# A query product with the cosine and sine parts stacked in its rows instead of a block-diagonal one

## The chip, the cores and the metric

One core of a Trainium2 chip runs the whole program. The metric is device time in microseconds, the median of the timed runs. PE is TensorE (PEld its weight loads), DVE VectorE, ACT ScalarE, POOL GpSimd and SP SyncE, which here issues DMAs.

## The reference, cut to what matters

The program is two decoder layers: RWKV mixing, a cross-attention over 1601 context rows and a mixture of experts, then grouped attention, a latent cross-attention and a second mixture. The change lies in the first cross-attention. What it computes for its queries:

```
q_hk  = (hidden_q @ Wq.T).reshape(B, S, H=16, K=128)
q_big = einsum('bshk,hkq->bshq', q_hk, w_kc_q)            # 192 dims a head
q_big = q_big * cos_q + rotate_half(q_big) * sin_q
q_r   = einsum('bshq,hqr->bhsr', q_big, W_qr)              # 64 dims a head
k_r   = einsum('bld,hdr->bhlr', kv_r, W_kr)
scores = einsum('bhsr,bhlr->bhsl', q_r, k_r)
```

The kernel folds Wq with w_kc_q (W1) and W_qr with W_kr (W2), so that the scores are a product of a 64-dim query per head with kv_r itself. The rotation is turned round: instead of rotating the 192 dims and multiplying by W2, it multiplies them by cosines and sines and uses W2 and W2 with its halves exchanged.

## The kernel before

**Heads go in pairs.** There are 8 pairs. A pair's 2 x 192 = 384 dims lie in three tiles of 128 partitions: tile 0 is the first 128 dims of its first head, tile 1 the first 128 of its second, tile 2 the last 64 of the first head (partitions 0 to 63) and the last 64 of the second (64 to 127). The tokens, 1024, go in two halves of 512 columns. So there are 16 jobs, n = 2 x pair + half.

**A job.** `z_jobs(n)` on PE makes the three tiles (`z`) in a bank each, from W1 and the normalised x, both split into a high and a low part (three products each, and two blocks of 128 channels: 18 products of 128x128 by 512). `rotate(n)` on DVE reads each bank and writes `zc` = z times cosine and `zs` = z times sine. `q_job(n)` on PE makes the query of both heads in one bank: partitions 0 to 63 are the first head's, 64 to 127 the second's. For tiles 0 and 1 it uses products of half the array's width (64 columns), one per head and part. For tile 2, which holds both heads, it uses `W2[:, p, c, 128:256]`, a 128x128 block-diagonal matrix, once with `zc` and once with `zs`. ACT copies the query's high part into `QALL`, `lows(n)` on DVE subtracts it and leaves the low part in `qlo`, and SP moves that by DMA into the other half of `QALL`'s partitions.

**The order.** Each engine's instructions are in the order of the program. On PE it is z(0), then z(n+1), q(n) for each n, with the turned keys (`first_keys`) ahead of q(14). On DVE it is rotate(0), then rotate(n+1), lows(n), with four low parts of the keys behind rotate(15). PSUM has 8 banks, taken in turn; a job waits until the one 8 banks back has been emptied.

**How W2 is made** (the end of the first stage, lines 615 to 629 and 1241 to 1254). `W2E` holds, for each pair, the product of W_kr and W_qr with 192 dims and the first 32 again, so that both the plain and the exchanged half are slices of it. For each pair PE turns two slices of 128 columns and, with four small products with the identity, puts the two heads' last 64 dims on the diagonal. ACT copies this out in three pieces per pair, four pairs ahead of `deviations(1, 1)` (the root for the second half of the layer norm) and four behind it. POOL has cleared the rest of the block-diagonal part with a memset. Then PE turns the normalised x (`turn_x(1)`), ACT takes its high part (`z_HTh`) and DVE its low part (`z_HTl`), all engines meet (`ended`), and the jobs start.

After the 16 jobs comes the unit stage (scores, softmax, context for 32 units), whose first scores wait for the last queries.

Of the kernel before, what the change touches and what calls it, by code (L numbers as in the profile page):

```python
# [13 lines left out]
P = 128  # L14
# [5 lines left out]
ALU = mybir.AluOpType  # L20
ACT = mybir.ActivationFunctionType
# [10 lines left out]
D = 64  # L32
H = 16
PAIRS = H // 2
QW = 192
# [51 lines left out]
def decoder(nc, x, ctx_512, L0_attn_Wk, L0_attn_Wv, L0_attn_Wr, L0_attn_Wo, L0_attn_time_decay, L0_attn_time_first,  # L87
# [5 lines left out]
    with ExitStack() as ctx:  # L93
# [5 lines left out]
        def sem(name):  # L99
            return ctx.enter_context(nc.semaphore(name))  # L100
# [12 lines left out]
        def at(name, offset, shape, dt=F32):  # L113
            size = int(np.prod(shape[1:])) * 4
            assert offset + size <= room, (name, offset + size, room)
            return nc.alloc_sbuf_tensor_at(name, shape, dt, offset=arena + offset)
# [38 lines left out]
        WkrT = at("WkrT", 40960, [D, H * D])  # L155
        x_woT = at("x_woT", 145152, [P, H, C])
        W1 = at("W1", 65536, [P, KC, H * QW])
        W2 = at("W2", 104480, [P, PAIRS, 2, 256])
        cosq = at("cosq", 129056, [P, 3, HALF])
        sinq = at("sinq", 135200, [P, 3, HALF])  # L160
        zc = at("zc", 141344, [P, 2, 3, HALF])
# [212 lines left out]
        w_exp = sem("rwkv_exp_ready")  # L374
        decay_exp = sem("decay_exp_ready")
        rw_ready = sem("rwkv_mixed")
        w2_cleared = sem("folded_weights_cleared")
        decay_set = sem("decays_ready")
        scan_step = sem("decayed_sums_ready")
        eps_added = sem("denominators_guarded")  # L380
# [126 lines left out]
        def _(pe):  # L507
            def begin(key, by):
                ps = banks.claim(key, by)
                if banks.earlier(key) is not None:  # L510
                    pe.wait_ge(*banks.emptied(banks.earlier(key)))
                return ps
# [103 lines left out]
            for t in range(NT):  # L616
                out_product(("ro", t), [(r_num[:, ct, t * P:(t + 1) * P], r_wt[:, 3, ct, :]) for ct in range(KC)])
            pe.wait_ge(*banks.emptied(("w2t", 3)))
            for p in range(PAIRS):
                ps = begin(("w2", p), "act")  # L620
                for c, (whole, rest) in enumerate(((0, P), (QW // 2, 32))):
                    o = 256 * c
                    nc.tensor.transpose(ps[:, o:o + P], W2E[:, p, whole:whole + P], ident[:, :])  # L623
                    for s in range(2):
                        rows = slice(s * D, (s + 1) * D)
                        last = mm(ps[rows, o + P + s * D:o + P + (s + 1) * D], W2E[rows, p, rest:rest + D], ident[rows, rows])
                last.then_inc(filled, 1)
            turn_x(1)
            ended(pe, 1)

# [10 lines left out]
            def q_job(n):  # L641
                p, half, s = n // 2, n % 2, n % 2
                pe.wait_ge(*banks.emptied(("z", p, half, 2)))
                ps = begin(("q", p, half), "dve")
                for c, r in enumerate((zc, zs)):
                    mm(ps[0:64, :], W2[:, p, c, 0:64], r[:, s, 0, :], c == 0, False, skip_group_check=True)
                    mm(ps[64:128, :], W2[:, p, c, 64:128], r[:, s, 1, :], c == 0, False, skip_group_check=True)
                for c, r in enumerate((zc, zs)):
                    last = mm(ps, W2[:, p, c, 128:256], r[:, s, 2, :], False, c == 1, skip_group_check=True)
                last.then_inc(filled, 1)  # L650

            def first_keys():

# [6 lines left out]
                    last.then_inc(filled, 1)  # L660

            wait_ht(1)
            banks.start_at(len(banks.order) % 8 + 4)
            z_jobs(0)
            for n in range(2 * PAIRS):
                if n + 1 < 2 * PAIRS:
# [488 lines left out]
        def _(act):  # L1155
# [82 lines left out]
            for g in range(4):  # L1238
                copy_out(("u", g), U[:, 2 * g:2 * g + 2, :])

            def folded(pairs):
                for p in pairs:
                    ps = banks.take(("w2", p), "act")
                    act.wait_ge(*banks.filled(("w2", p)))
                    src = ps.rearrange("p (c w) -> p c w", c=2)
                    nc.scalar.activation(W2[:, p, :, 0:P], src[:, :, 0:P], ACT.Copy)
                    nc.scalar.activation(W2[0:D, p, :, P:P + D], src[0:D, :, P:P + D], ACT.Copy)
                    nc.scalar.activation(W2[D:P, p, :, P + D:256], src[D:P, :, P + D:256], ACT.Copy).then_inc(emptied["act"], 1)

            deviations(1, 0)  # L1250
            act.wait_ge(w2_cleared, 1)
            folded(range(0, 4))
            deviations(1, 1)
            folded(range(4, PAIRS))
            for g in range(2):
                for kc in range(KC):
                    act.wait_ge(*banks.filled(("ht", 1, g, kc)))
# [214 lines left out]
        def _(dve):  # L1472
# [8 lines left out]
            V = nc.vector  # L1481
# [87 lines left out]
            def rotate(n):  # L1569
                p, half, s = n // 2, n % 2, n % 2  # L1570
                for j in range(3):
                    key = ("z", p, half, j)
                    ps = banks.take(key, "dve")
                    dve.wait_ge(*banks.filled(key))
                    if n >= 2:
                        dve.wait_ge(*banks.filled(("q", (n - 2) // 2, n % 2)))
                    V.tensor_tensor(zc[:, s, j, :], ps, cosq[:, j, :], ALU.mult)
                    V.tensor_tensor(zs[:, s, j, :], ps, sinq[:, j, :], ALU.mult).then_inc(emptied["dve"], 1)

            def lows(n):  # L1580
                p, half, s = n // 2, n % 2, n % 2
# [416 lines left out]
        def _(pool):  # L1998
# [19 lines left out]
            for ct in range(KC):  # L2018
# [1 line left out]
                for half in range(2):  # L2020
                    pool.wait_ge(*banks.emptied(("kvr", 2, ct, half)))
                G.tensor_tensor(r_sig[:, ct, :], r_num[:, ct, :], r_sig[:, ct, :], ALU.mult).then_inc(gated, 1)
            pool.wait_ge(*banks.emptied(("xwo", 7)))
            G.memset(W2[:, :, :, P:2 * P], 0.0).then_inc(w2_cleared, 1)

            def split(p):
                wide, narrow = slice(0, 2 * P), slice(2 * P, 3 * P)
                src = W1[:, :, 3 * P * p:3 * P * (p + 1)].rearrange("p k (h q) -> p k h q", h=2)
# [353 lines left out]
```

## Time and profile before

| | us |
|---|---|
| median of 3 runs | 1364.19 |
| lowest and highest | 1359.41, 1368.82 |
| span of the profiled execution | 1379.6 |
| PE busy in it | 1272.7 (92%) |
| DVE busy | 868.2 (63%) |
| POOL busy | 824.0 (60%) |
| ACT busy | 634.6 (46%) |

### The profile page before, as it was taken

What the parts mean: (1) busy time and instruction counts of PE and PEld (TensorE: products, weight loads), DVE (VectorE), ACT (ScalarE), POOL (GpSimd) and SP (SyncE); (2) the same over time, 40 slices, a digit from 0 to 9 for tenths busy, and PEclk for the clock granted to TensorE, in tenths of its full rate; (3) what the DMA queues carried; (4) which work ended last, traced back from release to release, by engine and by line L of the source; (5) the groups of instructions that cost most, each with busy time, mean ns of one, the idle gap of its engine ahead of it and who ended that gap; (6) DMA issues with size and microseconds to landing.
All of it is one profiled execution on the core that took longest, in us unless ns stands there. A gap on an engine that the chain in (4) does not pass through costs nothing.

```text
span 1379.6 us, 20358 instructions
## 1 busy us (share of the span) xinstructions
PE 1272.7 (92%) x7123; PEld 826.8 (60%) x7123; DVE 868.2 (63%) x1490; ACT 634.6 (46%) x1687; POOL 824.0 (60%) x748
## 2 busy tenths in 40 slices
PE   7999997999999999999999758998999999989792
PEld 4865554666666666666668643445776874556582
DVE  4756666677777777778865636675666123664443
ACT  3731123445554455544551416887665115872151
POOL 1267005799999999999993445887444004560444
PEclk9999997999999999999999888999999997998897
DMA  9501111000000000000005620000000105200263
GB/s 261 134 9 32 37 31 27 9 8 9 9 11 10 9 9 9 10 11 9 9 5 176 195 65 2 1 1 1 1 1 1 27 1 155 63 1 32 69 142 118
DMA packets 66172, 58.91 MB, mean 43 GB/s; under 512 B 19424, under 2 KB 62968, under 8 KB 65560
## 3 DMA queue, kind: packets, MB, share of 16 engines
q1 hardware_dynamic: 62952, 49.09, 12.7%
q0 software_dynamic: 3120, 8.52, 2.6%
q8 instruction: 58, 0.95, 0.3%
q14 instruction: 42, 0.34, 0.1%
HBM read 40.69 MB, written 8.52 MB: 36 GB/s over the span
## 4 chain that ended last, share of the span: by engine, by line
PE 79%; DVE 6%; ACT 5%; POOL 4%; issue 4%; DMA 1%; DVEq 0%; SPq 0%; POOLq 0%; ACTq 0%
PE PS L515 73%; PE PS L523 5%; ACT s_sc L1402 2%; POOL a_m L2137 2%; POOL a_m L2131 2%; DVE s_mx L1859 1%; ACT a_m L1356 1%; DVE pm L1622 1%; DVE HN L1504 0%; PE PS L729 0%; DMA f_xg<-token_rows,f_ids 0%; POOL s_sc L2152 0%; PE PS L685 0%; POOL f_xg L2119 0%; PE PS L623 0%
## 5 line engine op out<-in xcount | busy, mean ns | idle before, releaser
L2080 POOL TENSOR_TENSOR PWS<-PWS 128x1024 f32<-128x1024 f32 x160 | 379.7, 2373 | 45.1 <-ACT PWS L1286 25.8
L1622 DVE TENSOR_REDUCE pm<-PS 128x2 f32<-128x1024 f32 x192 | 225.8, 1218 | 69.3 <-PE PS L515 68.7
L1286 ACT ACTIVATE PWS<-PS 128x512 f32<-128x512 f32 (+1 forms) x416 | 213.3, 599 | 78.4 <-PE PS L515 78.2
L515 PE MATMUL PS<-PWS,KVR 128*64 128x256 f32 (+1 forms) x1664 | 185.8, 380 | 0.0
L515 PE MATMUL PS<-QALL,KH 128*128 128x512 f32 (+1 forms) x416 | 182.6, 439 | 0.9 <-DVE QM L1646 0.9
L515 PE MATMUL PS<-QM,KL 68*128 68x512 f32 (+1 forms) x416 | 167.3, 402 | 0.0
L2152 POOL TENSOR_SCALAR s_sc<-s_sc,s_ri 128x128 f32<-128x128 f32 (+1 forms) x256 | 104.5, 429 | 98.9 <-DVE s_ri L1866 98.9
L515 PEld LDWEIGHTS PS<-PWS,KVR 128*64 128x64 f32 (+1 forms) x1664 | 121.4, 137 | 59.0 <-issue 0.9
L515 PEld LDWEIGHTS PS<-QALL,KH 128*128 128x128 f32 (+1 forms) x416 | 77.9, 187 | 76.9 <-ACT PWS L1286 57.4
L1402 ACT ACTIVATE s_sc<-PS,s_nb 128x128 f32<-128x128 f32 (+1 forms) x256 | 104.5, 433 | 3.9 <-DVE s_nb L1862 3.9
L1859 DVE TENSOR_REDUCE s_mx<-PS 128x2 f32<-128x512 f32 (+2 forms) x112 | 65.7, 611 | 50.1 <-PE PS L515 50.0
L515 PE MATMUL PS<-KH,QALL 64*128 64x512 f32 (+1 forms) x512 | 89.3, 408 | 7.0 <-DVE pm L1622 7.0
L515 PE MATMUL PS<-a_wT,HT 128*128 128x512 f32 x192 | 93.4, 620 | 0.7 <-issue 0.7
L1297 ACT ACTIVATE QALL<-CTX 128x256 fp32r<-128x256 f32 x32 | 13.3, 417 | 154.0 <-DVE CTX L1659 154.0
L515 PEld LDWEIGHTS PS<-QM,KL 68*128 68x128 f32 (+1 forms) x416 | 79.0, 190 | 6.2
L515 PEld LDWEIGHTS PS<-KH,QALL 64*128 64x128 f32 (+1 forms) x512 | 46.9, 189 | 43.7 <-issue 26.0
L515 PE MATMUL PS<-z_HTh,z_w 128*128 128x512 f32 x192 | 67.5, 420 | 2.4 <-DVEq L502 2.4
L2180 POOL DMA_INDIRECT e_x<-token_rows,e_ids x31 | 29.5, 951 | 67.2 <-DVE e_ids L1956 46.8
L2131 POOL TENSOR_TENSOR a_m<-a_m,a_m 128x512 f32<-128x512 f32 x40 | 51.0, 1276 | 29.5 <-DVE a_m L1836 29.5
L1271 ACT ACTIVATE QALL<-PS 64x512 fp32r<-64x512 f32 x32 | 19.0, 594 | 106.3 <-PE PS L515 105.9
L1525 DVE TENSOR_TENSOR X<-X,PS 128x256 f32<-128x256 f32 x40 | 16.8, 419 | 76.8 <-PE PS L515 76.7
L1390 ACT ACTIVATE s_pt<-PS 128x512 f32<-128x512 f32 x64 | 38.5, 602 | 53.6 <-PE PS L523 53.6
(328 smaller groups left out, 2518.3 us busy)
## 6 DMA issues: line engine op xcount, KB each, us to landing
QALL<-qlo SPq DMA_DIRECT2D x32, 128.0 KB, 2.4
QM<-QALL SPq DMA_DIRECT2D x64, 64.0 KB, 2.0
f_w<-in_L_ffn_w_dram SPq DMA_DIRECT2D x2, 2048.0 KB
tile_results<-e_y SPq DMA_DIRECT2D x31, 128.0 KB
a_nat<-in_L_attn_w_qkv_dram SPq DMA_DIRECT2D x1, 3072.0 KB, 13.0
x_wq<-in_L_xattn_Wq_dram SPq DMA_DIRECT2D x1, 2048.0 KB, 10.4
x_wo<-in_L_xattn_Wo_dram SPq DMA_DIRECT2D x2, 1024.0 KB, 6.9
a_wo<-in_L_attn_w_o_dram SPq DMA_DIRECT2D x1, 2048.0 KB, 17.5
```

Source lines behind the costliest of these rows:

```text
L515: return nc.tensor.matmul(o, a, b, start=start, stop=stop, **kw)
L523: last = nc.tensor.transpose(ps[0:w, c:c + r], a, ident[0:r, 0:r])
L1286: nc.scalar.activation(PW[c][0:rows, j * HALF:(j + 1) * HALF], st_bank("block", LT * u + lt)[0:rows, :], ACT.Exp).then_inc(p_ready, 1)
L1390: nc.scalar.activation(s_pt[:, m % 2, 0, :], ps, ACT.Copy).then_inc(emptied["act_turned"], 1)
L1402: ins = nc.scalar.activation(s_sc[:, k % 4, h, 0:nk], ps[:, j * nk:(j + 1) * nk], ACT.Exp, bias=s_nb[:, k % 3, h:h + 1], scale=scale, accu ...
L1622: V.tensor_reduce(pm[u % 2][:, :, i // 3, i % 3], src, AX, ALU.max).then_inc(nat_read, 1)
L1859: ins = V.tensor_reduce(s_mx[:, k % 3, i * per:(i + 1) * per], banks.bank(key)[:, 0:per * nk].rearrange("p (h k) -> p h k", h=per), AX, AL ...
L2080: G.tensor_tensor(ACC[:, :], PW[0][:, :] if i == 0 else ACC[:, :], PW[i + 1][:, :], ALU.add).then_inc(acc_step, 1)
L2131: G.tensor_tensor(a_m1[:, n % 6, :], a_m1[:, n % 6, :], a_m2[:, n % 2, :], ALU.add).then_inc(m_sum, 1)
L2137: G.tensor_tensor(m1, m1, a_bt[:, i, s, :].unsqueeze(1).to_broadcast([P, 4, P]), ALU.add).then_inc(qk_ready, 1)
L2152: ins = G.tensor_scalar(s_sc[:, n % 4, h, 0:nk], s_sc[:, n % 4, h, 0:nk], s_ri[:, n % 4, h:h + 1], 1.0, ALU.mult, ALU.mult)
L2180: G.indirect_dma_start(e_x[:, j % 8, :], None, xs1, IndirectOffsetOnAxis(ap=e_ids[:, j:j + 1], axis=0)).then_inc(tile_back[j % 8], 16)
```

## The change

The last two products of `q_job`, of full width, become two of half width. Each head has its own weights for tile 2, with 128 rows: 64 for the cosine part and 64 for the sine part (`W2R[:, head, p, :]`). So the second index of `zc` and `zs` at tile 2 changes its meaning: `zc[:, s, 2, :]` holds the first head's cosine part in partitions 0 to 63 and its sine part in 64 to 127, and `zs[:, s, 2, :]` the second head's. `rotate` writes them with four instructions on 64 partitions each, two of which write other partitions than they read. W2's turned slices are made four to a bank and copied out whole, the small products write two banks of their own (one per head, cosine above sine), and the memset goes. `banks.start_at(4)` gives the same first bank as the expression that it replaces.

```
             for t in range(NT):
                 out_product(("ro", t), ...)
             pe.wait_ge(*banks.emptied(("w2t", 3)))
+            for g in range(4):
+                turn(("w2", g), "act", [W2E[:, p, whole:whole + P] for p in (2 * g, 2 * g + 1) for whole in (0, QW // 2)])
+            rests = [begin(("w2r", s), "act") for s in range(2)]
             for p in range(PAIRS):
-                ps = begin(("w2", p), "act")
-                for c, (whole, rest) in enumerate(((0, P), (QW // 2, 32))):
-                    o = 256 * c
-                    nc.tensor.transpose(ps[:, o:o + P], W2E[:, p, whole:whole + P], ident[:, :])
-                    for s in range(2):
-                        rows = slice(s * D, (s + 1) * D)
-                        last = mm(ps[rows, o + P + s * D:o + P + (s + 1) * D], W2E[rows, p, rest:rest + D], ident[rows, rows])
-                last.then_inc(filled, 1)
+                for s, ps in enumerate(rests):
+                    rows = slice(s * D, (s + 1) * D)
+                    for c, rest in enumerate((P, 32)):
+                        last = mm(ps[c * D:(c + 1) * D, p * D:(p + 1) * D], W2E[rows, p, rest:rest + D], ident[rows, rows])
+            last.then_inc(filled, 2)
...
-                for c, r in enumerate((zc, zs)):
-                    last = mm(ps, W2[:, p, c, 128:256], r[:, s, 2, :], False, c == 1, skip_group_check=True)
-                last.then_inc(filled, 1)
+                mm(ps[0:64, :], W2R[:, 0, p, :], zc[:, s, 2, :], False, True, skip_group_check=True)
+                mm(ps[64:128, :], W2R[:, 1, p, :], zs[:, s, 2, :], False, True, skip_group_check=True).then_inc(filled, 1)
...
             deviations(1, 0)
-            act.wait_ge(w2_cleared, 1)
-            folded(range(0, 4))
+            for g in range(4):
+                copy_out(("w2", g), W2[:, 2 * g:2 * g + 2, :, :])
             deviations(1, 1)
-            folded(range(4, PAIRS))
+            for s in range(2):
+                copy_out(("w2r", s), W2R[:, s, :, :])
...
-                    V.tensor_tensor(zc[:, s, j, :], ps, cosq[:, j, :], ALU.mult)
-                    V.tensor_tensor(zs[:, s, j, :], ps, sinq[:, j, :], ALU.mult).then_inc(emptied["dve"], 1)
+                    if j < 2:
+                        V.tensor_tensor(zc[:, s, j, :], ps, cosq[:, j, :], ALU.mult)
+                        V.tensor_tensor(zs[:, s, j, :], ps, sinq[:, j, :], ALU.mult).then_inc(emptied["dve"], 1)
+                        continue
+                    for h, both in enumerate((zc, zs)):
+                        mine = slice(h * D, (h + 1) * D)
+                        V.tensor_tensor(both[0:D, s, j, :], ps[mine, :], cosq[mine, j, :], ALU.mult)
+                        ins = V.tensor_tensor(both[D:P, s, j, :], ps[mine, :], sinq[mine, j, :], ALU.mult)
+                    ins.then_inc(emptied["dve"], 1)
...
-            pool.wait_ge(*banks.emptied(("xwo", 7)))
-            G.memset(W2[:, :, :, P:2 * P], 0.0).then_inc(w2_cleared, 1)
```

## Rows read from the trace of the kernel before

**Rows 1.** The page, chain that ended last, share of the span by engine.

```profile
PE 79%; DVE 6%; ACT 5%; POOL 4%; issue 4%; DMA 1%; DVEq 0%; SPq 0%; POOLq 0%; ACTq 0%
```

**Rows 2.** Busy time by stretches (stretch, length, PE, PEld, DVE, ACT, POOL, clock, DMA).

```profile
82.00:210.00 128.00, 127.92 (x495) 74.33 (x497) 81.80 (x130) 19.60 (x35) 47.86 (x49) 1.00 0.14 29
```

**Rows 3.** Timeline of DVE and ACT in the jobs (start, duration, engine, line, operation).

```profile
97.68 0.68 DVE L1578 TENSOR_TENSOR zs<-PS,sinq 128x512 f32<-128x512 f32 x1
98.28 0.68 DVE L1577 TENSOR_TENSOR zc<-PS,cosq 128x512 f32<-128x512 f32 x1
...
100.07 0.68 DVE L1578 TENSOR_TENSOR zs<-PS,sinq 128x512 f32<-128x512 f32 x1
...
102.23 1.21 ACT L1271 ACTIVATE QALL<-PS 64x512 fp32r<-64x512 f32 x2 [6.62 <-PE PS L515]
...
103.47 1.39 DVE L1589 TENSOR_TENSOR qlo<-PS,QALL 64x512 fp32r<-64x512 f32 x2 [2.73 <-ACT QALL L1271]
...
110.12 1.21 ACT L1271 ACTIVATE QALL<-PS 64x512 fp32r<-64x512 f32 x2 [6.67 <-PE PS L515]
```

**Rows 4.** Timeline of PE over the query products of job 1.

```profile
98.34 1.08 PE L515 MATMUL PS<-zc,W 128*64 128x512 f32 x4
99.25 1.03 PE L515 MATMUL PS<-zs,W 128*64 128x512 f32 x4
100.21 1.12 PE L515 MATMUL PS<-zc,W 128*128 128x512 f32 x2
...
102.26 0.40 PE L515 MATMUL PS<-z_HTl,z_w 128*128 128x512 f32 x1
```

**Rows 5.** Timeline of PE's weight loads there.

```profile
101.60 0.19 PEld L515 LDWEIGHTS PS<-z_HTh,z_w 128*128 128x128 f32 x1 [0.24 <-issue]
102.03 0.19 PEld L515 LDWEIGHTS PS<-z_HTl,z_w 128*128 128x128 f32 x1 [0.24 <-issue]
```

**Rows 6.** Timeline of PE, turned keys and query products of jobs 14 and 15.

```profile
200.78 1.53 PE L659 MATMUL PS<-ident,DUP 128*128 128x128 f32 x13
...
202.24 1.08 PE L515 MATMUL PS<-zc,W 128*64 128x512 f32 x4
...
206.02 1.08 PE L515 MATMUL PS<-zc,W 128*64 128x512 f32 x4
```

**Rows 7.** Line 1646, DVE's row maxima (durations in ns, least, median, most).

```profile
L1646 DVE TENSOR_TENSOR QM<-PS,ident x32: 681/682/683, 219.9 to 710.0; 4x512 fp32r<-4x512 f32 x32
```

**Rows 8.** The chain that ended last in order of time, folded weights.

```profile
70.01 0.26 PE PS L623
70.27 0.26 PE PS L515 x4
```

**Rows 9.** Timeline of the end of the first stage.

```profile
72.40 0.36 DVE L1498 BATCH_NORM_AGGREGATE mv<-stats 128x2 f32<-128x6 f32 x4
74.55 0.30 ACT L1171 ACTIVATE rstd<-mv,guard 128x4 f32<-128x4 f32 x1
75.10 1.38 DVE L1504 TENSOR_SCALAR HN<-X,mv,rstd 128x256 f32<-128x256 f32 x4
77.75 1.97 PE L523 MATMUL PS<-ident,HN 128*128 128x128 f32 x16
79.35 2.48 DVE L1565 TENSOR_TENSOR z_HTl<-PS,z_HTh 128x512 fp32r<-128x512 f32 x4 [2.87 <-ACT z_HTh L1258]
```

**Rows 10.** Timeline of PE, products of 64 rows by 64 columns.

```profile
56.12 2.82 PE L515 MATMUL PS<-WqrT,WkrT 64*64 64x192 f32 x32
```

**Rows 11.** Groups of instructions from 58 to 69.2 us.

```profile
L1167 ACT ACTIVATE U<-PS 128x512 f32<-128x512 f32 x4 | 2.4, 622 | 0.5 <-PE PS L515 0.5
```

**Rows 12.** Busy time by stretches, columns as in rows 2.

```profile
80.00:82.00 2.00, 0.00 (x0) 0.00 (x0) 1.83 (x4) 0.78 (x2) 0.06 (x1) 1.00 0.00 0
...
214.00:216.00 2.00, 0.56 (x2) 0.29 (x2) 1.97 (x3) 0.00 (x0) 1.63 (x3) 0.50 0.27 57
...
230.00:232.00 2.00, 2.00 (x8) 1.43 (x7) 0.00 (x0) 1.57 (x3) 1.86 (x2) 0.79 0.00 0
```

More of the change, by code:

```diff
@@ L157, in decoder @@
         W1 = at("W1", 65536, [P, KC, H * QW])
-        W2 = at("W2", 104480, [P, PAIRS, 2, 256])
+        W2 = at("W2", 104480, [P, PAIRS, 2, P])
+        W2R = at("W2R", 112672, [P, 2, PAIRS, D])
         cosq = at("cosq", 129056, [P, 3, HALF])
@@ L376, in decoder @@
         rw_ready = sem("rwkv_mixed")
-        w2_cleared = sem("folded_weights_cleared")
         decay_set = sem("decays_ready")
@@ L662, in _ @@
             wait_ht(1)
-            banks.start_at(len(banks.order) % 8 + 4)
+            banks.start_at(4)
             z_jobs(0)
@@ L1239, in _ @@
                 copy_out(("u", g), U[:, 2 * g:2 * g + 2, :])
[L1241 to L1248, printed above, removed]
             deviations(1, 0)
-            act.wait_ge(w2_cleared, 1)
-            folded(range(0, 4))
+            for g in range(4):
+                copy_out(("w2", g), W2[:, 2 * g:2 * g + 2, :, :])
             deviations(1, 1)
-            folded(range(4, PAIRS))
+            for s in range(2):
+                copy_out(("w2r", s), W2R[:, s, :, :])
             for g in range(2):
```

## The prediction

> **What bounds the kernel now.** I began with the chain that ended last. TensorE (PE) holds 79% of the span, so an edit pays if it shortens PE's own work where PE is that chain [rows 1]. Then the table by stretches: from 82 to 210 us, where the queries are made (call it the query stage), PE is busy 127.92 of 128.00 us at a granted clock of 1.00, while VectorE (DVE) has 81.80, ScalarE (ACT) 19.60 and GpSimd (POOL) 47.86 [rows 2]. The other three engines have room there and PE has none. Last, the timeline of one job, and that of the end of the stage before, from 69 to 82 us.
>
> The query stage is 16 jobs. ACT's copy of a finished query starts at 102.23 and again at 110.12, so a job lasts 7.89 us [rows 3]. On PE a job is 18 rotation-input products (z) and one query product group (q).
>
> Before, a job has two pairs and two full-width products, eight slots. After, it has three pairs, six slots. The new pair is of the same shape as those of the row (128 rows by 64 columns, two different moving tiles, one bank). Gain: 2 x 0.43 = 0.86 a job. The changeover from half to full width moves from inside q to between q and z, at the same price. At the end q jobs 14 and 15 stand one behind the other, 3.78 us apart (202.24 to 206.02) [rows 6]; there eight slots are 3.44 and the other 0.34 is two changeovers, most of which goes, and half of it goes behind the last job. Sum: 16 x 0.86 = 13.8, and 0.4, is 14.2 us.
>
> **What DVE pays.** The rotation by cosine and sine is six instructions of 128x512 a job. They start 0.60 us apart (97.68, 98.28) though one lasts 0.68: neighbours overlap. The two low-part instructions of 64x512 take 1.39 together, so these don't overlap: 0.69 each [rows 3]. After, the third z has four instructions of 64x512 where it had two of 128x512. I bound one by the row nearest in shape, 0.69 without overlap, and by 0.60 with it. Two of the four read 64 partitions and write the other 64. The one row that moves partitions is that of the row maxima, from partitions 0 to 3 into 64 to 67, 512 elements: 0.682 us, no dearer [rows 7]. DVE's job: 4 x 0.60 and 4 x 0.69 and 1.39 and two gaps of 0.03, 6.6 us, against 5.0 before. PE's job will be 7.89 - 0.86 = 7.03. DVE still waits 0.4 us a job for ACT, where it waited 2.73 (100.07 plus 0.68, to 103.47). Nor does it delay PE by order: rotation n+2 follows the low parts of n, which start 1.44 behind q job n, and so ends 1.44 + 6.6 = 8.0 us after it, while q job n+2 needs it 7.03 + 4.1 = 11.1 after it. So I cost DVE at nothing; the cover is 3 us of lead, and 0.4 us a job by throughput. If the cover goes, each 0.1 us of DVE's excess is 1.6 us in all.
>
> The Trainium skill (VectorE: DVE Perf Modes, Two Vector instructions with no wait between them) speaks against the change here: an instruction whose input or output starts in another group of 32 partitions than that of its neighbour starts only when everything earlier has finished. The trace agrees: 0.69 for the low parts, which step from partition 0 to 64, and 0.60 for the rotations. By it three of the four new instructions are held, as I have them; without it DVE's job would be 6.25 us.
>
> The end of the query stage is tighter. Counted from the start of the last z job, that is the end of q job 13, the last rotation ends at 1.44 + 1.39 + 5.2 = 8.0. PE has the z job (7.89 less the 3.69 from 98.34 to 102.03, 4.2), the turned keys (202.24 less 200.78, 1.46, [rows 6]) and q job 14 (six slots, 2.6) before q job 15, which it could start at 8.3. I charge nothing and keep 0.3 in the range.
>
> **The folded weights, 69 to 82 us.** PE alternates between a 128x128 turn, 0.26 us on the chain, and a group of four 64x64 records, 0.26 too, 16 times: 8.3 us [rows 8]. Two turns of x's halves, 16 records, take 1.97 [rows 9]: 0.12 apiece, so 0.14 of each 0.26 is the change of shape. After, the 16 turns stand together: 16 x 0.12 = 1.9. The 64 small records stand together as well. From below: 32 records of 64x192 take 2.82 us [rows 10], 0.088 each, a third of that for 64 columns is 0.03, so 1.9 us. From above: 0.26 per four, 4.2 us. The lower is nearer, since 0.26 holds the change of shape; I take 2.4. PE would then be through at 69.4 + 1.9 + 2.4 = 73.7 instead of 77.7.
>
> It doesn't all come out, for what is late next is the second half of the normalised rows. DVE has its variances at 72.76 and then waits until ACT, in the midst of its folded copies, turns to them at 74.55; the rows are written from 75.10 to 76.48 [rows 9]. After, ACT has four copies of 128x512 (0.622 each, [rows 11]) instead of twelve small ones: from 70.0 to 72.5, so the deviation goes at 72.8, the rows are ready at 74.7, PE's last turns end at 75.8, ACT's last high part at 76.9 and DVE's last low part at 77.7, where it was 79.35 + 2.48 = 81.83 [rows 9]. That is 4.1. With the small records at 4.2, PE ends them at 75.5, ACT's two copies of the rest follow, and the chain ends at 80.0: 1.8. I take 3.4, nearer to the first. The removed memset on POOL lay at 58.5 and kept nobody waiting: nil. No DMA is touched.
>
> **Sum.** 14.2 + 3.4 = 17.6 us of a span of 1379.6. The page gives the profiled execution's span alone; it is 15.4 above the median of the runs, 1364.19, and I carry the difference over: 1346.6. All that follows the query stage waits for PE's last q job or for what hangs on it and is the same code, so it moves up whole. What may differ is the clock there: the unit stage opens with gaps on PE and at 214 to 216 us the granted clock is 0.50, that is 1.2 GHz [rows 12]. How long it stays depends on how the gaps fall; the runs differ by 9 us with one kernel, and I put +-4 on it.
>
> **The rivals.**
> 1. *The third pair doesn't share its slots.* Then six half-width products cost eight slots, only the folded weights pay: 1364.2 - 3.4 = 1360.8. Against it stand the two pairs of [rows 4], of the same shape; for it, only that this pair closes the sum. 0.07.
> 2. *The clock falls before the query stage.* PE would now idle for the rows at 74 and again until 78. Before, it stood idle from 79.7 until DVE's last low part at 81.83 and the clock at 80 to 82 was 1.00 [rows 9, 12], which speaks against. In the unit stage it stayed at half from 214 to 231, 17 us; as much here costs 8.5: 1355. 0.08. [...]
> 3. *DVE becomes the bound, and the kernel slower.* The mechanism is the two instructions a job that move between partition halves. Beside them DVE's job is 6.6 - 1.4 = 5.2 us. It bounds above 7.03, so from 0.9 us for such an instruction. The kernel is slower than before when a job is 0.2 (the 3.4 of the first stage over 16) above 7.89, so from 1.4. At 1.8: 8.8 a job, 0.9 above, 16 x 0.9 - 3.4 = 11 slower, 1375. [rows 7] say 0.68 for a move of 64 partitions, but of four rows only, not of 64. 0.05. Short of that point, with DVE bound at 0.9 to 1.4, 1347 to 1361: 0.05.
> 4. *It does as said, and the sum holds*: 0.75, with 1341 to 1352 as its own range: the folded weights give -1.6 or +0.7, the last rotation 0.3, the clock and the median of few runs the rest.
>
> **Chances and range.** A measurement of this kernel can tell about 1%, 13.6 us, from no change: below 1350.5 is faster. Of case 4 nine tenths lie there, 0.68. Within 1%: the rest of 4, rivals 1 and 2, DVE bound short of slower, 0.27. Slower: 0.05. The range reaches from 1340 to 1356, case 4 and rival 2 with the nearer part of 3.
>
> **What would show it.** In the query stage ACT's query copies 7.03 us apart, not 7.9; in a q job twelve half-width records in six slots and no full-width one; DVE's four 64x512 instructions 0.69 apart and 0.3 to 0.5 us of waiting for ACT left before the low parts. In the first stage the 16 turns in 1.9 us and the last low part at 77.7 to 80. Wrong if a slot holds one half-width record in the new pair, if DVE's wait for ACT is gone, if the granted clock between 74 and 195 is under 1, or if the unit stage lengthens by what the query stage loses.

## The result, and the profile after

The changed kernel takes 1344.26 us (median of 4 runs, 1343.50 to 1354.52). The kernel before, on the same chip, takes 1366.51 (4 runs, 1359.41 to 1370.50). The ratio is 0.9869, 95% interval 0.9839 to 0.9900: 17.9 us of 1364, where 17.6 were forecast. It is not the quotient of the two medians, which is 0.9837, or 22.3 us; all ratios below are of this kind, and those of e1 to e4 leave out two executions of the kernel before that took 1822 and 3142 us. The profiled execution took 1343.5 us, with a span of 1341.7.

I read the two traces at landmarks first. Both kernels have the same code up to the folded weights and again from the first score product (KH by QALL) on. In the profiled executions these are the first z product, 82.08 before and 76.87 after, and the first score product, 209.80 and 193.46. So the first stage gave 5.2 us. Of these 0.8 are not the change's: PE starts the folded weights at 69.48 before and at 68.70 after, and the difference is there already at the first product of x_kcq by x_wq (38.64 and 37.86), in code that both share. The query stage went from 127.72 to 116.59, 11.1 less. From there to the end the code is the same. The two spans differ by 37.9, more than the medians do. The unit stage is 2.1 shorter, and the 19.5 that are left lie behind it, where the clock was lower in the profiled execution before: 0.68 from 1160 to 1180 us, 0.74 from 1260 to 1280 and 0.76 from 1300 to 1320, while the same code after, 18 to 38 us earlier, shows 1.00, 0.96 and 1.00. That part is none of the change's, and only the ratio of many runs is used for the whole.

In the chain that ended last PE holds 78% of the span, where it held 79% [rows 1].

PE over the query products of job 1 in the kernel after (the timeline; start, duration, engine, line, operation). It answers to [rows 4]:

```profile
95.18 1.08 PE L515 MATMUL PS<-zc,W 128*64 128x512 f32 x4
...
96.94 0.59 PE L515 MATMUL PS<-zc,W2R 128*64 128x512 f32 x1
...
96.95 0.59 PE L515 MATMUL PS<-zs,W2R 128*64 128x512 f32 x1
...
97.37 0.59 PE L515 MATMUL PS<-zc,W2R 128*64 128x512 f32 x1
97.38 0.59 PE L515 MATMUL PS<-zs,W2R 128*64 128x512 f32 x1
...
97.90 0.50 PE L515 MATMUL PS<-z_HTh,z_w 128*128 128x512 f32 x1
98.24 0.39 PE L515 MATMUL PS<-z_HTl,z_w 128*128 128x512 f32 x1
```

The third pair is seen at once: its records start two by two, 0.01 us apart, and the next two 0.43 later. From the first query record to the second z product of the next job it is 3.06 us (95.18 to 98.24), with twelve half-width records. Before it was 3.92 (98.34 to 102.26 [rows 4]), with eight half-width and four full-width ones: 0.86 more, two slots.

DVE and ACT in the same job (timeline of the kernel after), which answer to [rows 3]:

```profile
95.50 0.68 DVE L1570 TENSOR_TENSOR zs<-PS,sinq 128x512 f32<-128x512 f32 x1
...
96.10 0.67 DVE L1574 TENSOR_TENSOR zc<-PS,cosq 64x512 f32<-64x512 f32 x1
...
96.79 0.69 DVE L1575 TENSOR_TENSOR zc<-PS,sinq 64x512 f32<-64x512 f32 x1
...
97.48 0.69 DVE L1574 TENSOR_TENSOR zs<-PS,cosq 64x512 f32<-64x512 f32 x1
...
98.02 1.21 ACT L1262 ACTIVATE QALL<-PS 64x512 fp32r<-64x512 f32 x2 [5.78 <-PE PS L515]
98.19 0.69 DVE L1575 TENSOR_TENSOR zs<-PS,sinq 64x512 f32<-64x512 f32 x1
...
99.26 1.39 DVE L1587 TENSOR_TENSOR qlo<-PS,QALL 64x512 fp32r<-64x512 f32 x2 [0.37 <-ACT QALL L1262]
...
105.06 1.21 ACT L1262 ACTIVATE QALL<-PS 64x512 fp32r<-64x512 f32 x2 [5.84 <-PE PS L515]
```

ACT's copies stand 7.04 us apart (98.02, 105.06), where it was 7.89. The four new instructions start 0.69 to 0.71 apart, and DVE still waits 0.37 for ACT (0.43 in the next job), where it waited 2.73. So PE is still the bound, but with a twentieth of a job to spare. The two of L1575 and L1574 that move 64 partitions to the other half cost no more than the two that don't.

The seam at the end, PE's query products 14 and 15 and the first scores, and DVE's last instruction of rotation 15 (timelines of the kernel after), answers to [rows 6]:

```profile
188.16 1.08 PE L515 MATMUL PS<-zc,W 128*64 128x512 f32 x4
...
189.74 0.69 DVE L1575 TENSOR_TENSOR zs<-PS,sinq 64x512 f32<-64x512 f32 x1
...
190.79 1.03 PE L515 MATMUL PS<-zc,W 128*64 128x512 f32 x4
...
193.46 0.87 PE L515 MATMUL PS<-KH,QALL 64*128 64x512 f32 x4
```

Job 15 follows job 14 after 2.63 us instead of 3.78. PE doesn't wait for the last rotation, which ends at 190.43, 0.36 before job 15 starts.

The end of the first stage in the kernel after (timeline), which answers to [rows 8, 9]:

```profile
68.70 1.91 PE L523 MATMUL PS<-ident,W2E 128*128 128x128 f32 x16
...
70.54 1.16 PE L515 MATMUL PS<-ident,W2E 64*64 64x64 f32 x64
...
71.63 0.36 DVE L1489 BATCH_NORM_AGGREGATE mv<-stats 128x2 f32<-128x6 f32 x4
71.64 1.09 PE L523 MATMUL PS<-ident,HN 128*128 128x128 f32 x8
72.02 0.30 ACT L1170 ACTIVATE rstd<-mv,guard 128x4 f32<-128x4 f32 x1 [0.62 <-DVE mv L1489]
...
72.57 1.38 DVE L1495 TENSOR_SCALAR HN<-X,mv,rstd 128x256 f32<-128x256 f32 x4
...
74.01 1.09 PE L523 MATMUL PS<-ident,HN 128*128 128x128 f32 x8 [1.28 <-DVE HN L1495]
...
75.33 1.29 DVE L1556 TENSOR_TENSOR z_HTl<-PS,z_HTh 128x512 fp32r<-128x512 f32 x2 [0.18 <-ACT z_HTh L1249]
...
76.87 0.76 PE L515 MATMUL PS<-z_HTh,z_w 128*128 128x512 f32 x1 [1.77 <-DVEq L502]
```

The 16 turns take 1.8 us (forecast 1.9) and the 64 small records 1.1 in all. PE has done the first eight turns of x's rows at 72.7. Then it stands twice, 1.28 us before the other eight and 1.77 before z. What is late now is DVE: its variances at 71.99, the rows from 72.57, the last low part from 75.33. ACT waits 0.62 for DVE there, and not DVE for ACT.

In the second of these waits, at 76.2 us, the clock fell. Busy time by stretches of the kernel after, columns as in [rows 2]:

```profile
74.00:76.00 2.00, 1.09 (x8) 0.86 (x8) 1.82 (x4) 1.35 (x3) 0.00 (x0) 1.00 0.00 0
76.00:78.00 2.00, 1.13 (x3) 0.97 (x4) 0.62 (x2) 0.00 (x0) 1.13 (x3) 0.54 0.00 0
78.00:80.00 2.00, 2.00 (x7) 1.51 (x6) 0.10 (x1) 0.00 (x0) 2.00 (x3) 0.50 0.00 0
80.00:82.00 2.00, 2.00 (x6) 1.61 (x5) 1.19 (x2) 0.00 (x0) 1.86 (x3) 0.50 0.00 0
82.00:84.00 2.00, 2.00 (x8) 1.52 (x8) 1.29 (x2) 0.00 (x0) 2.00 (x3) 0.75 0.00 0
84.00:86.00 2.00, 2.00 (x11) 1.63 (x9) 1.84 (x3) 0.00 (x0) 2.00 (x3) 1.00 0.00 0
86.00:188.00 102.00, 102.00 (x442) 59.95 (x441) 95.03 (x147) 17.24 (x30) 38.95 (x39) 1.00 0.18 37
```

The first z products run at 1.2 GHz until 83 us: PE is busy all the time, with 6 or 7 records in 2 us where it has 11 from 84 on. In the one profiled execution of the kernel before nothing of it is there, though PE stood still from 80 to 82 [rows 12]. This is rival 2, in a short form.

### The profile page after: what moved, and what is told of

It reads as the page before. It is cut to its first block, busy times and chain, and to the rows that moved or that the text cites. A ratio compares the mean times of both kernels' runs of the same rounds, so it can differ in the third digit from the quotient of the medians.

```text
span 1341.7 us, 20371 instructions
## 1 busy us (share of the span) xinstructions
PE 1241.2 (93%) x7123; PEld 811.9 (61%) x7123; DVE 890.9 (66%) x1522; ACT 630.1 (47%) x1669; POOL 821.2 (61%) x747
## 4 chain that ended last, share of the span: by engine, by line
PE 78%; DVE 6%; ACT 6%; POOL 5%; issue 3%; DMA 2%; DVEq 0%; POOLq 0%; SPq 0%; ACTq 0%
PE PS L515 72%; PE PS L523 5%; ACT s_sc L1393 2%; POOL a_m L2132 2%; POOL a_m L2126 2%; DVE s_mx L1857 2%; ACT a_m L1347 1%; POOL e_yg L2180 1%; DVE pm L1620 1%; DVE HN L1495 1%; PE PS L728 0%; DVE stats L1485 0%; DMA f_xg<-token_rows,f_ids 0%; POOL s_sc L2147 0%; ACT PWS L1277 0%
## 5 line engine op out<-in xcount | busy, mean ns | idle before, releaser
L1277 ACT ACTIVATE PWS<-PS 128x512 f32<-128x512 f32 (+1 forms) x416 | 212.7, 600 | 76.7 <-PE PS L515 75.2
L1653 DVE RECIPROCAL PS<-PS 128x256 f32<-128x256 f32 x32 | 55.9, 1747 | 6.6 <-PE PS L515 6.6
```

What stands on the lines that cost most here:

```text
L1277: nc.scalar.activation(PW[c][0:rows, j * HALF:(j + 1) * HALF], st_bank("block", LT * u + lt)[0:rows, :], ACT.Exp).then_inc(p_ready, 1)
L1653: V.reciprocal(sums, sums).then_inc(inv_ready, 1)
```

## The experiments

All were run beside the kernel before; times of different rows need not be from the same chip, so compare ratios. e1 to e4 are from one chip, e5 to e8 from a second, and e9 to e11 and the row of before from a third. e1 gives the last 64 dims of each head other weights, and e9 leaves out the stacking of the cosine and sine parts, so their queries are not the reference's. "z" is the start of the first z product; "stage" is from there to the first score product; "half" is how long the granted clock was 0.50 between 74 and 84 us. z, stage and half are of the one profiled execution.

| run | time (runs) | ratio, 95% | z | stage | half |
|---|---|---|---|---|---|
| before | 1364.02 (11) | | 82.1 | 127.7 | 0 |
| after | 1344.26 (4) | 0.9869, 0.9839 to 0.9900 | 76.9 | 116.6 | 6.8 |
| e1_wide_again | 1361.37 (10) | 0.9982, 0.9954 to 1.0010 | 76.9 | 129.1 | 3.4 |
| e2_columns_apart | 1360.28 (1) | | 75.9 | 129.2 | 3.4 |
| e3_shapes_mixed | 1349.29 (10) | 0.9903, 0.9871 to 0.9935 | 78.7 | 115.3 | 3.4 |
| e4_filled_gaps | 1340.16 (4) | 0.9818, 0.9763 to 0.9873 | 77.4 | 113.7 | 0 |
| e5_dve_one_more | 1346.63 (1) | | 75.4 | 121.1 | 3.4 |
| e6_dve_two_more | 1364.25 (1) | | 75.7 | 133.4 | 0 |
| e7_again | 1345.53 (4) | 0.9870, 0.9799 to 0.9941 | 76.2 | 115.1 | 3.4 |
| e8_filled_both | 1342.68 (4) | 0.9823, 0.9761 to 0.9886 | 75.5 | 113.7 | 0 |
| e9_old_rotation | 1350.00 (1) | | 75.3 | 113.7 | 0 |
| e10_filled_gaps | 1340.62 (5) | 0.9821, 0.9798 to 0.9845 | 77.5 | 113.7 | 0 |
| e11_again | 1344.77 (6) | 0.9857, 0.9835 to 0.9879 | 75.2 | 115.3 | 3.4 |

z itself lies between 75.2 and 76.9 for identical code (after, e7, e11), by differences that are there when PE starts the folded weights (68.70, 68.05, 67.01). From there to z it is 8.16 or 8.17 us in each of them, and 12.60 before.

**The folding alone: full-width products again.**

```diff
-                mm(ps[0:64, :], W2R[:, 0, p, :], zc[:, s, 2, :], False, True, ...)
-                mm(ps[64:128, :], W2R[:, 1, p, :], zs[:, s, 2, :], False, True, ...).then_inc(filled, 1)
+                for c, r in enumerate((zc, zs)):
+                    last = mm(ps, W2[:, p, c, :], r[:, s, 2, :], False, c == 1, ...)
+                last.then_inc(filled, 1)
```

> The changed kernel, with the last two products of a query job of full width again, on the turned slices of W2 (so the last 64 dims of each head get wrong weights); the folding of the weights and the rotation on VectorE stay as changed. If a pair of half-width products costs what one full-width product does, and the end of the first stage gives the rest, a job lasts 7.9 us instead of 7.04, the query stage is 14 us longer than in the changed kernel, and the time is 4 to 5 us below before: ratio to before about 0.997. Rival, that the gain came from the first stage and from where the clock falls: within 3 us of the changed kernel.

Measured: 1361.37, ratio 0.9982, and a stage of 129.07. The difference to the changed kernel is what the third pair saves on PE. It has to be taken at the same clock. In e1 the clock was at half for 3.4 us, as in e7 and e11, which are the changed kernel too (115.05 and 115.27): 13.8 to 14.0 us in the stage, as expected. The changed kernel's first profile, with 6.8 us at half, would give 12.5. By the two ratios (0.9982 less 0.9869 of 1364) it is 15.4 in the whole. The folding alone shows as 1.4 us by the medians and 2.5 by the ratio, where 4 to 5 were expected; the interval (0.9954 to 1.0010) takes in both no gain and the 4.4 less 1.4 to 1.6 for the clock.

**The pairs taken apart: three products of one half, then three of the other.**

```diff
                 for c, r in enumerate((zc, zs)):
                     mm(ps[0:64, :], W2[:, p, c, 0:64], r[:, s, 0, :], ...)
-                    mm(ps[64:128, :], W2[:, p, c, 64:128], r[:, s, 1, :], ...)
                 mm(ps[0:64, :], W2R[:, 0, p, :], zc[:, s, 2, :], ...)
+                for c, r in enumerate((zc, zs)):
+                    mm(ps[64:128, :], W2[:, p, c, 64:128], r[:, s, 1, :], ...)
                 mm(ps[64:128, :], W2R[:, 1, p, :], zs[:, s, 2, :], ...)
```

> The changed kernel, the six half-width products of a job in another order: the three of columns 0 to 63, then the three of columns 64 to 127. If a half-width product is cheap because its neighbour in the other columns shares its slots, the sharing is lost but for the seam: 11 to 12 slots of 0.43 us instead of 6, a job of 9.2 to 9.7 us, the query stage 35 to 42 us longer. If a product of 64 columns is cheap in itself, no change.

A miss: the job became 7.98 us, two slots longer, and not four to six. PE over one job's query products (timeline of this kernel):

```profile
101.74 1.07 PE L515 MATMUL PS<-zc,W 128*64 128x512 f32 x2
102.65 0.59 PE L515 MATMUL PS<-zs,W 128*64 128x512 f32 x1
102.65 0.64 PE L515 MATMUL PS<-zc,W 128*64 128x512 f32 x1
103.08 0.59 PE L515 MATMUL PS<-zs,W 128*64 128x512 f32 x1
103.13 0.59 PE L515 MATMUL PS<-zc,W 128*64 128x512 f32 x1
103.50 0.59 PE L515 MATMUL PS<-zc,W2R 128*64 128x512 f32 x1
...
104.42 1.02 PE L515 MATMUL PS<-zs,W2R 128*64 128x512 f32 x2
```

The first product of columns 64 to 127 (the zc record at 102.65) stands behind all three of columns 0 to 63 in the program. It starts before the third of them (W2R, 103.50) and before the second one's second record (103.08). Only the first and the last product stand alone, eight slots in all. So slots are shared here too, by products that aren't neighbours in the program but use different columns. Why the first product isn't shared as well isn't shown. Eight slots of half-width products cost what eight slots with full-width ones do (stage 129.2 beside 129.07, both with the clock at half for 3.4 us), which is the slot count confirmed from the other side.

The Trainium skill (TensorE: Matmul & The Clock Gate, Part 3: Packing small matmuls — row/col tiling) has products start in program order, "strict FIFO, no reordering". These rows differ by 0.43 and 0.85 us, and the measurement decides.

**Turns and small products mixed again, in the new buffers.**

```diff
-            for g in range(4):
-                turn(("w2", g), "act", [W2E[:, p, whole:whole + P] for p in (2 * g, 2 * g + 1) ...])
+            wholes = [begin(("w2", g), "act") for g in range(4)]
             rests = [begin(("w2r", s), "act") for s in range(2)]
             for p in range(PAIRS):
+                for c, whole in enumerate((0, QW // 2)):
+                    o = (p % 2 * 2 + c) * P
+                    turned = nc.tensor.transpose(wholes[p // 2][:, o:o + P], W2E[:, p, whole:whole + P], ident[:, :])
+                if p % 2:
+                    turned.then_inc(filled, 1)
                 for s, ps in enumerate(rests):
```

> The changed kernel, TensorE alternating again for each pair between the two 128x128 turns and the four small products, with the same banks and copies as changed. If 0.14 us of each 0.26 was the change of shape, the folding takes 16 changes: two turns 0.37 and eight small records 0.3 a pair, 8 x 0.67 = 5.4 us instead of 2.9; the deviation still comes early, so what is seen at the start of the query stage is 1 to 2 us, ratio to the changed kernel under 1.002. If small records cost 0.065 each however they stand, the folding of the changed kernel would have lasted 5.9, which its trace has not.

PE and ACT in this kernel (timeline), two of the eight pairs and what comes behind the last:

```profile
71.61 0.44 PE L624 MATMUL PS<-ident,W2E 128*128 128x128 f32 x2
71.98 0.34 PE L515 MATMUL PS<-ident,W2E 64*64 64x64 f32 x8
...
72.25 0.44 PE L624 MATMUL PS<-ident,W2E 128*128 128x128 f32 x2
...
73.37 0.60 ACT L1170 ACTIVATE W<-PS 128x512 f32<-128x512 f32 x1 [0.69 <-PE PS L624]
...
73.86 0.29 ACT L1174 ACTIVATE rstd<-mv,guard 128x4 f32<-128x4 f32 x1
```

Two turns and their eight small records take 0.64 (71.61 to 72.25), 5.1 us for the eight pairs, where standing apart they take 2.9 (from 68.70 to 71.64 in the rows of after). ACT's last copy comes at 73.37 and its deviation at 73.86, where it was at 72.02, and z is at 78.70. From the start of the folded weights to z it is 10.3 us here, 8.2 after and 12.6 before. So putting each kind together, against mixing them by pairs, is worth 2.1 of the folding's 4.4 us. The edit costs another 1.1: it takes all six banks ahead of the first turn, and so PE starts the folding later, after a wait of 0.96 for DVE.

This is not yet the order of before, which changed shape four times a pair (1.04 us) and not twice. No run isolates what makes the other 2.3. ACT's fewer and larger copies did not bring the deviation forward: it comes 5.4 us behind the start of the folding here and came 5.1 behind it before. What is shorter is the way from the deviation to z, 4.8 us here and 7.5 before, where PE was still at the folding until 77.75.

The whole kernel came out at 0.9903, 0.0034 above the changed kernel's ratio, where less than 0.002 was expected (0.0034 of 1364 is 4.6 us, and 2.1 and 1.1 are 3.2). The two intervals overlap, so the whole tells no difference for sure.

**PE's two waits filled with products that nobody reads.**

```diff
-            turn_x(1)
+            turn_x(1, (0,))
+            pe.wait_ge(*banks.emptied(("w2", 3)))
+            mm(banks.bank(("w2", 3)), W1[:, 0, 0:P], W1[:, 0, 0:HALF])
+            turn_x(1, (1,))
+            for i in range(3):
+                mm(banks.bank(("w2", 3))[:, 0:256], W1[:, 0, 0:P], W1[:, 0, 0:256])
```

> The changed kernel with one product of 512 columns and three of 256 put into TensorE's two waits at the end of the first stage (results not used). If the clock fell at 76 us because TensorE stood idle for 1.3 and 1.8 us there, it stays at 1.00 up to the unit stage, the first z jobs run at full speed, and 2.5 to 3 us are gained on the changed kernel (ratio to before about 0.984). If the clock falls for another reason, nothing is gained or up to 0.3 us are lost.

Busy time by stretches in this kernel, columns as before:

```profile
76.00:78.00 2.00, 1.53 (x8) 1.01 (x7) 1.15 (x2) 0.32 (x1) 0.68 (x2) 1.00 0.00 0
```

The clock stays at 1.00, and the stage is 113.7: 14.0 less than before, and 2.9 less than in the changed kernel. The 14.0 are the third pair without the clock, the 2.9 the clock's price in the execution with 6.8 us at half. z isn't later for the added products: 8.16 us from the start of the folded weights, as without them.

**One and two more DVE instructions a job.** They write a buffer that nobody reads; the first line is e5, both are e6.

```diff
                         ins = V.tensor_tensor(both[D:P, s, j, :], ps[mine, :], sinq[mine, j, :], ALU.mult)
+                    ins = V.tensor_tensor(spare[0:D, s, :], ps[D:P, :], sinq[D:P, j, :], ALU.mult)
+                    ins = V.tensor_tensor(spare[D:P, s, :], ps[D:P, :], sinq[D:P, j, :], ALU.mult)
```

> The changed kernel with one instruction more on VectorE in each rotation, a fifth of 64x512 that writes a place nobody reads. VectorE's job becomes 6.6 + 0.7 = 7.3 us against TensorE's 7.04, so by the sum its 0.4 us of waiting are gone and it bounds by 0.26 us a job: over 14 jobs, less the slack of 0.2 to 0.3 at the end, the query stage from the first z product to the first scores is 3 to 4 us longer than in the changed kernel. Rival, that VectorE has more room than the sum says (its lead of 3 us covers it): no change.

> The same with two more. VectorE's job is 8.0 us, 0.95 above TensorE's: the query stage 12 to 14 us longer than in the changed kernel, which gives back nearly all that the third pair gained, and TensorE's wait for the rotation shows before the query products. Rival as before: less than 3 us.

ACT and PE with one more (timeline):

```profile
123.46 1.21 ACT L1263 ACTIVATE QALL<-PS 64x512 fp32r<-64x512 f32 x2 [5.84 <-PE PS L516]
...
130.51 1.21 ACT L1263 ACTIVATE QALL<-PS 64x512 fp32r<-64x512 f32 x2 [5.84 <-PE PS L516]
...
134.99 1.08 PE L516 MATMUL PS<-zc,W 128*64 128x512 f32 x4 [0.21 <-DVE spare L1577]
...
137.84 1.21 ACT L1263 ACTIVATE QALL<-PS 64x512 fp32r<-64x512 f32 x2 [6.12 <-PE PS L516]
...
142.34 1.08 PE L516 MATMUL PS<-zc,W 128*64 128x512 f32 x4 [0.24 <-DVE spare L1577]
...
193.78 1.08 PE L516 MATMUL PS<-zc,W 128*64 128x512 f32 x4 [3.04 <-DVE spare L1577]
```

With two more:

```profile
163.53 1.08 PE L516 MATMUL PS<-zc,W 128*64 128x512 f32 x4 [0.94 <-DVE spare L1578]
...
203.81 1.98 PE L516 MATMUL PS<-zc,W 128*64 128x512 f32 x4 [3.75 <-DVE spare L1578]
```

With one more, DVE's wait for ACT is gone, but the first jobs still take 7.05 us (ACT's copies at 123.46 and 130.51, and those before alike). Only from the copy at 137.84 on is a job 7.35 and does PE wait for DVE. Until then DVE's lead covers what it is behind, so the expectation's rival is right for the first half of the stage. The lead only puts the payment off. Against the changed kernel, seven jobs are 0.3 longer, 2.1 us; job 14's copy comes another 0.4 later and job 15's 3.3, for there PE has no z job between the last two query jobs and stands for DVE's whole delay (3.04 us before job 15). That makes 5.8 of the 5.9 by which the stage grew (121.1 against 115.2 at the same clock); 3 to 4 were expected.

With two more the job is 8.06 from ACT's fourth copy on. The stage grew by 19.7 (133.4 against 113.7), where 12 to 14 were expected: 11.7 in the jobs, 1.1 before job 14 and 6.6 at job 15, of which 3.75 are PE's wait and most of the rest is a clock at half behind it (four records in 1.98 us instead of 1.08).

So the margin that I claimed is measured in the stage: with 0.4 us a job left the change is free, 0.3 beyond it costs 6 us, 1.0 beyond costs all that it brought. Of the whole kernel there is one execution each. e6's 1364.25 is as long as before; e5's 1346.63 is only 1.1 above e7's median on the same chip, with a unit stage of 510.6 us beside 515.0 in e7's profile, so the whole can't confirm the 6.

**The changed kernel again, and both openings filled.** The second also gives PE products that nobody reads where the unit stage opens, up to eight after each of the first score products and three after two of the later steps.

```diff
+            def busy(k):
+                pe.wait_ge(*banks.emptied(("k", 0)))
+                for i in range(k):
+                    mm(PS[:, 2 * 512:3 * 512], KH[0][:, 0:P], KH[0][:, 0:HALF])
...
+                busy((0, 3, 2, 8, 1, 1)[n])
```

> The changed kernel itself, once more. Its time lies 1.3% below before (ratio 0.984 to 0.990), and if the fall of the clock at the end of the first stage is the rule and not an accident of one execution, the granted clock is 0.5 again for 5 to 7 us from 76 us.

> The changed kernel with filling products in both places: at the end of the first stage as in the run before, and in TensorE's waits at the opening of the unit stage (20 products of 512 columns between the first plain scores and the first turned ones, results not used). The granted clock was 0.5 there from 198.5 to 208.6 us. If it stays at 1.00, the twelve products of the first blocks run at 0.23 us instead of 0.43, 2.5 us, and what else ran slow gives up to 2 us more: 3 to 4.5 us below the kernel filled in one place, 6 to 7 below the changed one, ratio to before 0.979. If the products delay the chain through VectorE's maxima, nothing is gained.

The changed kernel repeats: 0.9870. The clock fell again, at 75.6 us, but for 3.4 us and not 5 to 7. With both filled, the clock held until 211.6 us instead of falling at 197 (e4) or 199 (the changed kernel's first profile), and then fell all the same, to 0.50 at 212 to 218. The unit stage, to the last score product (QALL by KH), took 509.4 us, where e4's took 510.5 and the changed kernel's profiles show from 510.5 to 515.0. The whole is 2.9 us below e7, where 6 to 7 were expected. Filling the second place brought nothing that these runs can tell.

**The rotation as before, with the third pair kept.**

```diff
-                    if j < 2:
+                    if j < 3:
```

> The changed kernel with the rotation of the third tile in its old form, two instructions of 128x512 instead of four of 64x512 (the cosine and sine parts are then not stacked, so the queries are wrong). VectorE's job falls from 6.6 to 5.0 us. If VectorE's four instructions cost nothing, as forecast, the query stage keeps its length (115 to 117 us with the clock's fall in it) and VectorE waits 1.9 us a job for ScalarE instead of 0.4. If they hold TensorE back, the stage is 1 to 4 us shorter.

DVE in this kernel (timeline):

```profile
122.97 1.39 DVE L1587 TENSOR_TENSOR qlo<-PS,QALL 64x512 fp32r<-64x512 f32 x2 [1.95 <-ACT QALL L1262]
```

DVE waits 1.95 us a job instead of 0.37, and the stage is 113.7, to the tenth what it is with the four new instructions and the clock at 1.00 (e4, e8, e10). They cost nothing. The kernel's 1350.0 is one execution in which the clock was lower later (unit stage 513.7 against 510.5), and says nothing on them.

**The filled kernel and the changed one, in five rounds on one chip.**

> The kernel filled at the end of the first stage, beside the changed kernel on one chip. The first z jobs run at 2.4 GHz; 2.5 to 3 us, 0.2%, below the changed kernel. Rival, that the gain at the start is lost later in the lottery of the clock: no difference.

> The changed kernel on the same chip as the run before: ratio to before 0.985 to 0.989, 0.002 above the filled kernel.

1340.62 and 1344.77: the filled kernel is 4.2 us below the changed one, 0.3%. The two intervals against before overlap (0.9798 to 0.9845, 0.9835 to 0.9879). Side by side the two kernels are told apart better: all five runs of the filled one (1339.24 to 1341.09) lie below all six of the changed one (1343.44 to 1349.42). The profiles show 1.6 us in the query stage and 1.1 in the unit stage; these two executions are 8.4 apart in the whole, so they don't divide up the 4.2 exactly. It is the best version that I ran.

## Why the prediction was right

**The third pair: right.** Forecast 14.2 us, measured 14.0 (127.72 to 113.7, in e4, e8, e9 and e10, where the clock doesn't disturb). The job is 7.04 where 7.03 was forecast. The step from eight slots to six is shown from both sides: with full-width products the stage is 13.8 to 14.0 longer at the same clock (e1), and with the pairs taken apart, which makes eight slots of half-width products, it is as long as with e1's eight (e2). Rival 1 is out.

**DVE at nothing: right, with the margin as given.** 0.37 us of waiting was left, 0.4 forecast. e9 shows the cost at nil, e5 and e6 show where it would begin. On the held start the Trainium skill (VectorE: DVE Perf Modes, Two Vector instructions with no wait between them) and the trace agree: the first of the four starts 0.60 behind its neighbour (95.50 to 96.10), and the three that follow, in other partitions, 0.69 to 0.71 apart. No run tells this from another reading, that instructions of 64 partitions don't overlap one another. By 0.60 there would have been 0.7 to spare, and one more instruction would have fitted into the job; it cost 6 us in the stage. Rival 3 is out at 0.69 an instruction, and its mechanism is real: e6 is as slow as the kernel before (1364.25).

**The end of the query stage at nothing: right.** No wait in front of job 15. The forecast was 0.3 us between the last rotation and PE, and it is 0.36 (190.43, 190.79). e5 shows what this is worth: 0.3 a job more, and PE stands there 3.0 us.

**The folded weights: the mechanism right, the size 1.0 too small.** Forecast 3.4, measured 5.2 less the 0.8 that are not the change's, 4.4. The text worked out 4.1 for short small records and 1.8 for long ones, and took 3.4 between them. The mis-sized term is the 64 small records: 2.4 us taken, bounded by 1.9 and 4.2, and they took 1.1, 0.017 each, below the lower bound. That bound came from 64x192 records [rows 10], divided as if time went by columns; why they took less isn't shown. So the pull towards 1.8 was not due. What was "late next" in the text then decided, the second half of the rows on DVE, nearly on time. To compare with the text's times, which start from 69.4, 0.8 has to be added to the trace's: the deviation at 72.8, as forecast, and the end of the last low part at 77.4, where the text had 77.7.

**The clock before the query stage: rival 2 came true, and cheaply.** Of the nine profiled executions after the change in which PE's waits weren't filled, the clock fell at 74 to 80 us in seven. In the three filled ones it never did; were they like the others, that would happen by chance about once in a hundred. I had given it 0.08, because PE had stood 2.4 us before without a fall [rows 9, 12], and priced it at 8.5 us from the unit stage, where the clock stayed down for 17. It stayed down for 3.4 in six of the seven and for 6.8 in the one profiled first, and cost 1.4 to 2.9 us (stages of 115.1 to 116.6 against 113.7). The error in the price was the length. It was carried over from a stretch with waits (PE busy 0.56 of 2.00 us at 214) to one where PE is busy all the time from z on; that this made the difference is my reading, and no run isolates it.

**The sum.** 14.0 + 4.4 - 1.4 is 17.0 for most executions, 15.5 for the one profiled first. The three measured ratios give 17.9, 17.7 and 19.5 us, each with some 3 to 10 either way. So the 17.6 is right in its main term, and two smaller errors, folding 1.0 too low and the clock 1.4 to 2.9 not counted, work against each other. That the total came so close is in part luck. The clock in the unit stage gave its own scatter: 510.4 to 515.1 us for the same code over all profiles, within the 4 that were put on it. Behind it the clock scatters as well, which the text left out: 19.5 us between the two profiled executions above, and 8.0 between those of e10 and e11 (granted clock 0.98 and 0.83 from 1240 to 1260 us).

**What stays open.** Why the clock fell in seven executions and not in e6 and e9: the two waits of e9, 1.28 and 1.77 us, are those of the changed kernel. What made the 2.3 of the folding's 4.4 us that e3 leaves. And 1.5 of the 4.2 us between the filled and the changed kernel.

## What to carry to other kernels

Count TensorE's time in slots, not in products: two half-width products in different columns cost here what one full-width product does. So where two block-diagonal products are summed, and half of their weights are zeros, stack what they multiply in the rows; one pair of half-width products then does the work of both. Then check the engine that prepares the moving tiles at two places, the average job and the last one: 0.4 us to spare held here, but what is missing comes out at once where the pipeline runs dry (3.0 us in front of the last job for 0.3 a job), while in the first jobs a lead hides it. And where a stage is shortened, look at PE's waits just ahead of a long full stretch: here 1.3 and 1.8 us of them cost 1.4 to 2.9 us of clock, and a few products that nobody reads took that back in three profiles of three.

## What the runs showed of the hardware that I had not expected

- Half-width products of other columns start ahead of program order: in e2 one starts at 102.65, beside the second product of the other columns and ahead of the third (103.50), behind which it stands in the program.
- 64 records of 64x64 by 64 columns, spread over the four quarters of the array, take 1.1 us, 0.017 each, where 64x192 ones take 0.088. Changing between these and 128x128 turns costs more than they do: per head pair 1.04 us with four changes (before), 0.64 with two (e3), 0.37 with each kind together (2.9 over 8), of which the eight small records are 0.14.
- Moving 64 partitions to the other half is free on DVE: 0.67 to 0.69 us with or without.
- Before the change PE stood still for 2.4 us and the clock held, in the one execution profiled. After it PE stood 1.28 and 1.77 us with 1.09 of turns between, and the clock fell in seven of nine, in the second wait or within 0.4 us behind it.
